# Query and key products of the first two batches straight from the loaded float32 data, for eight of sixteen heads

## The chip, the cores and the metric
The kernel runs on one core of a Trainium2 chip. Its time is device microseconds of one execution. The kernel before was timed three times; in addition, one execution was recorded by the hardware profiler, and all rows shown here come from that one.

## The reference
x is 8 batches of 128 tokens by 128 features, float32; ctx_1024 has the same shape. The computation is one decoder layer with layer norm behind each of its three parts:

```python
x = _layernorm(x + attn(x, w_q, w_k, w_v, w_o))             # 16 heads of 64, causal softmax(q k' / 8) v
x = _layernorm(x + xattn(x, ctx, mask, Wq..bo))             # 16 heads of 8, masked
x = _layernorm(x + ffn(x, router_w, w_gate, w_up, w_down))  # 8 experts, top 2, silu(gate) * up
```

The change touches only the first lines of the self-attention: `q = einsum(x, w_q)`, `k = einsum(x, w_k)`, `v = einsum(x, w_v)`, with weights of 1024 columns each (16 heads of 64), and the scale 1/8 of the scores, which the kernel multiplies into the query weights.

## The kernel before
All five engines run straight lists of instructions, written out by hand; semaphores tie them together, and there is no planner. TensorE works through its list in order, so what stands in front of an instruction delays it.

**Split products.** A product of x with the projection weights is made of three products in a rounded format. A float32 array a is held as a_hi, a rounded to the format float32r, and a_lo = a - a_hi. `split_product` (line 1441) adds hi*hi, lo*hi and hi*lo in one bank of PSUM. The three weight matrices are split in nine parts, `W_PARTS` (line 62): for each of the four column ranges of 256 (`W_COLS`) the query and then the key part, and last the value matrix as a whole. ScalarE makes the hi half with the scale in it (`round_w`, line 512, counted by `w_hi_done`), VectorE the lo half (`lower_w`, line 803, counted by `w_lo_done`), which reads the raw and the hi array in SBUF. GpSimd splits x pair by pair of batches (`split_x`, line 284).

**Loads.** SyncE issues xT of the first pair, one key part, three query parts, the value weights (line 254), the rest of xT (line 255), ctx and smaller ones; ScalarE issues the other weight parts (lines 508 to 510). Behind all lowerings (line 269) SyncE issues the gate and up weights, which overwrite the raw projection weights.

**The opening on TensorE** (from line 1609): ten float32 matmuls on a zeroed tile (`WARM`), then `first_qk(p)` for p = 0 to 7: q and k of two heads for the first pair of batches, each over 256 tokens, in one bank. `score_s(0, 0)`, the scores of eight heads of batch 0, stands behind `first_qk(5)`; it needs `first_qk(0)` to `(3)` copied out. Then follow `first_qk(6)`, `project_v(0, 0)`, `first_qk(7)`, `next_qk(0, 0)`, `project_v(0, 1)`, `next_qk(0, 2)`, `next_qk(0, 3)` and `score_s(0, 1)`. `next_qk(n, i)` is the same product for the next pair. Where a bank of PSUM is taken again, TensorE waits for its reader: `first_qk(7)` for `group_max("s", 0, 0)`, and `score_s(0, 1)` for `evac_v(0, 1)`.

**The copies out of PSUM.** ScalarE copies `first_qk` with even p (`evac_first_qk`, line 532), VectorE those with odd p (line 897). VectorE's list in this stage is: `lower_w(0)` to `(7)`, copies 1 and 3, `lower_w(8)`, two `group_max` (line 831, four masked reductions each), `evac_v(0, 0)`, copy 5, a reciprocal, copy 7, `evac_v(0, 1)`. ScalarE's is: `round_w(0)` to `(7)`, copies 0 and 2, `round_w(8)`, copy 4, a DMA issue, and the exponentials. GpSimd's is: `split_x(0)`, `split_x(1)`, `round_ctx(0)`, `split_x(2)`, `split_x(3)`, and then normalisations of the probabilities (line 311).

Of the kernel before, what the change touches and what calls it, by code (L numbers as in the profile page):

```python
# [38 lines left out]
def build_decoder(nc, x, xT, ctxT, mask, wqT, wkT, wvT, woT, cwqT, cwkT, cwvT, cwoT, cbq, cbk, cbv, cbo,  # L39
# [19 lines left out]


    W_COLS = (slice(0, 256), slice(256, 512), slice(512, 768), slice(768, 1024))
    W_PARTS = [(i, cols) for cols in W_COLS for i in (0, 1)] + [(2, slice(0, 1024))]
    NWP = len(W_PARTS)
    WARM = 10
    W_SCALE = (DQ ** -0.5, 1.0, 1.0)


# [6 lines left out]
    with ExitStack() as ctx:  # L74
# [3 lines left out]
        def sem(name):  # L78
            return ctx.enter_context(nc.semaphore(name))
# [130 lines left out]
        def hid_of(b):  # L210
            return max((j + 1 for j in range(NFILL) if FILL_BANK[j] is b), default=0)

        ld_xT, ld_xT_rest, ld_wv, ld_cwk, ld_cwq, ld_x, ld_ctx, ld_mask, ld_wo, ld_cw, ld_gu, ld_down = [
            sem(f"ld_{n}") for n in "xT xT_rest wv cwk cwq x ctx mask wo cw gu down".split()]
        stored, consts, pad_set, mask_set, w_hi_done, w_lo_done, gu_split, x_split, ctx_hi_done, ctx_lo_done, cwk_ready, cwq_ready, bias_step, bias_then_mean = [
            sem(n) for n in ("stored consts pad_set mask_set w_hi_done w_lo_done gu_split x_split ctx_hi_done ctx_lo_done cwk_ready cwq_ready "
                             "bias_step bias_then_mean").split()]
# [1 line left out]
            sem(n) for n in "qk_first qk_first_a qk_first_v kc_proj kc_evac kc_lower cv_proj cv_evac k_own_done cvp_done".split()]  # L219
        qk_proj, qk_evac = [[sem(f"{n}{i}") for i in range(4)] for n in ("qk_proj", "qk_evac")]  # L220
        v_proj, v_evac = [[sem(f"{n}{i}") for i in range(2)] for n in ("v_proj", "v_evac")]
        ld_wqk = [sem(f"ld_w{'qk'[i]}{k}") for k in range(len(W_COLS)) for i in (0, 1)]
        scored = {"s": [sem(f"scored_s{a}") for a in range(2)], "c": [sem(f"scored_c{j}") for j in range(NG)]}
        maxed, exped, turned, turned_evac = [{k: [sem(f"{n}_{k}{g}") for g in range(NG)] for k in "sc"}
                                             for n in ("maxed", "exped", "turned", "turned_evac")]
# [22 lines left out]
        @block.sync  # L248
        def _(sp):
            sp.dma_start(xT_all[:, 0:2 * S], xT[:, 0:2 * S]).then_inc(ld_xT, 16)  # L250
            sp.dma_start(w_raw[:, 1, W_COLS[0]], wkT[:, W_COLS[0]]).then_inc(ld_wqk[1], 16)
            for k in range(1, len(W_COLS)):
                sp.dma_start(w_raw[:, 0, W_COLS[k]], wqT[:, W_COLS[k]]).then_inc(ld_wqk[2 * k], 16)
            sp.dma_start(w_raw[:, 2, :], wvT).then_inc(ld_wv, 16)
            sp.dma_start(xT_all[:, 2 * S:B * S], xT[:, 2 * S:B * S]).then_inc(ld_xT_rest, 16)
            sp.dma_start(ctxT_all[:], ctxT).then_inc(ld_ctx, 16)
            sp.dma_start(cwqk_raw[:, 1], cwkT).then_inc(ld_cwk, 16)
            sp.dma_start(cwv_sb[:], cwvT).then_inc(ld_cw, 16)
            sp.dma_start(cwo_sb[:], cwoT).then_inc(ld_cw, 16)
            sp.dma_start(cb[:, 0], cbq).then_inc(ld_cw, 16)  # L260
            sp.dma_start(cb[:, 1], cbk).then_inc(ld_cw, 16)
            sp.dma_start(part[:], parts).then_inc(ld_cw, 16)
            sp.dma_start(cbrow[:, 0, :], cbv.rearrange("(a d) -> a d", a=1).broadcast_to([P, D])).then_inc(ld_cw, 16)
            sp.dma_start(cbrow[:, 1, :], cbo.rearrange("(a d) -> a d", a=1).broadcast_to([P, D])).then_inc(ld_cw, 16)
            sp.dma_start(router_sb[:], routerT).then_inc(ld_cw, 16)
            sp.dma_start(cwqk_raw[:, 0], cwqT).then_inc(ld_cwq, 16)
            sp.dma_start(wo_sb[:], woT).then_inc(ld_wo, 16)

            sp.wait_ge(w_lo_done, NWP)
            sp.dma_start(gu_raw[:, 0, :], gateT).then_inc(ld_gu, 16)  # L270
            sp.dma_start(gu_raw[:, 1, :], upT).then_inc(ld_gu, 16)
            sp.wait_ge(k_own_done, B)
            sp.dma_start(down_sb[:], down).then_inc(ld_down, 16)

            for c in range(NCH):
                for tb in range(TB):
                    b = c * TB + tb
                    sp.wait_ge(y_ready, b + 1)
                    sp.dma_start(out[b], y_out[:, tb, :]).then_inc(stored, 16)
            sp.wait_ge(stored, 16 * B)  # L280

        @block.gpsimd
        def _(pool):
            def split_x(k):
                toks = slice(2 * k * S, 2 * (k + 1) * S)
                pool.wait_ge(ld_xT if k == 0 else ld_xT_rest, 16)
                pool.tensor_copy(x_hi[:, toks], xT_all[:, toks]).then_inc(x_split, 1)
                pool.wait_ge(x_split, 2 * k + 1)
                pool.tensor_tensor(x_lo[:, toks], xT_all[:, toks], x_hi[:, toks].bitcast(F32), ALU.subtract).then_inc(x_split, 1)
# [217 lines left out]
        def _(act):  # L507
# [2 lines left out]
                act.dma_start(w_raw[:, 1, W_COLS[k]], wkT[:, W_COLS[k]]).then_inc(ld_wqk[2 * k + 1], 16)  # L510

            def round_w(part_of):
                i, cols = W_PARTS[part_of]
                act.wait_ge((*ld_wqk, ld_wv)[part_of], 16)
                act.activation(w_hi[:, i, cols], w_raw[:, i, cols], ACT.Copy, scale=W_SCALE[i]).then_inc(w_hi_done, 1)

            def exp(kind, g, n):
# [14 lines left out]
            def evac_first_qk(p, b):  # L532
                act.wait_ge(qk_first, p + 1)
                dst = qk_b[:, :, p % 4, :] if p >= 4 else qk_a[:, 0, :, p, :]
                act.copy(dst, b[:].rearrange("p (a c) -> p a c", a=2)).then_inc(qk_first_a, 1)

            def evac_qk(n, i, b):
                act.wait_ge(qk_proj[i], n + 1)
# [49 lines left out]
            def rank_exp():  # L588
                act.wait_ge(r_exp_in, 1)
                act.activation(r_a[:, 4:6].rearrange("p a b e -> p (a b e)"),  # L590
                               r_a[:, 0:2].rearrange("p a b e -> p (a b e)"), ACT.Exp).then_inc(r_exp, 1)

            round_w(0)
            round_w(1)
            round_w(2)
            round_w(3)
            round_w(4)
            round_w(5)
            round_w(6)
            round_w(7)  # L600
            evac_first_qk(0, Y1)
            evac_first_qk(2, T0)
            round_w(8)
            evac_first_qk(4, Y0)
            act.dma_start(mask_all, mask.rearrange("b q t -> q b t")).then_inc(ld_mask, 16)
            exp("s", 0, 0)
# [191 lines left out]
        def _(dve):  # L798
# [2 lines left out]
            dve.memset(cvp[:, :, :, DC:DC + 1], 1.0).then_inc(pad_set, 1)  # L801

            def lower_w(part_of):
                i, cols = W_PARTS[part_of]
                dve.wait_ge(w_hi_done, part_of + 1)
                dve.scalar_tensor_tensor(out=w_lo[:, i, cols], in0=w_raw[:, i, cols], scalar=W_SCALE[i],
                                         in1=w_hi[:, i, cols].bitcast(F32), op0=ALU.mult,
                                         op1=ALU.subtract).then_inc(w_lo_done, 1)
# [88 lines left out]
            def evac_first_qk(p, b):  # L897
                dve.wait_ge(qk_first, p + 1)
                dst = qk_b[:, :, p % 4, :] if p >= 4 else qk_a[:, 0, :, p, :]
                dve.tensor_copy(dst, b[:].rearrange("p (a c) -> p a c", a=2)).then_inc(qk_first_v, 1)  # L900

            def evac_qk(n, i, b):
                dve.wait_ge(qk_proj[i], n + 1)
# [139 lines left out]
            def rank_9():  # L1043
                step(tt(hot1, hot1, wide(z1), ALU.mult))
                step(tt(hot2, hot2, wide(z2), ALU.mult))
                tt(dense_w[:], hot1, hot2, ALU.add).then_inc(dense_ready, 1)

            lower_w(0)
            lower_w(1)
            lower_w(2)  # L1050
            lower_w(3)
            lower_w(4)
            lower_w(5)
            lower_w(6)
            lower_w(7)
            evac_first_qk(1, OS)
            evac_first_qk(3, T1)
            lower_w(8)
            dve.wait_ge(consts, 3)
            group_max("s", 0, 0, Y1)  # L1060
            group_max("s", 1, 0, T1)
            evac_v(0, 0, OS)
            evac_first_qk(5, X0)
            reciprocal_s(0, 0)
# [375 lines left out]
        def _(pe):  # L1440
# [11 lines left out]
                return last  # L1452

            def first_qk(p, b):
                if p == 0:

                    for a in range(2):
                        dst, cols = b[:, a * 2 * S:(a + 1) * 2 * S], slice(0, P)
                        pe.wait_ge(w_hi_done, a + 1)
                        pe.wait_ge(x_split, 1)  # L1460
                        pe.matmul(dst, w_hi[:, a, cols], x_hi[:, 0:2 * S], start=True, stop=False)
                        pe.wait_ge(x_split, 2)
                        pe.matmul(dst, w_hi[:, a, cols], x_lo[:, 0:2 * S], start=False, stop=False)
                        pe.wait_ge(w_lo_done, a + 1)
                        last = pe.matmul(dst, w_lo[:, a, cols], x_hi[:, 0:2 * S], start=False, stop=True)
                    last.then_inc(qk_first, 1)
                    return
                if p % 2 == 0:
                    pe.wait_ge(w_lo_done, p + 2)
                project_qk(0, p, b).then_inc(qk_first, 1)  # L1470

            def next_qk(n, i, b):
# [645 lines left out]
```

## Time and profile before

| | us |
|---|---|
| median of three runs | 233.56 (233.28 to 233.65) |
| the profiled execution: time / span | 233.06 / 231.0 |
| TensorE busy in the span | 225.9 (98%) |
| VectorE / ScalarE / GpSimd busy | 192.1 / 164.9 / 102.0 |

The span runs from the first to the last instruction of the program; the time of the same execution holds 2.06 us more around it. The profile's page says in how much of the span each engine was busy, and which line's work made up the chain that ended last. A float32 matmul stands in the trace as two records (the ten opening matmuls are 20 records), a float32r matmul as one. The granted share of TensorE's clock is 1.00 in every stretch of the run.

### The profile page before, as it was taken

What the parts mean: (1) busy time and instruction counts of PE and PEld (TensorE: products, weight loads), DVE (VectorE), ACT (ScalarE), POOL (GpSimd) and SP (SyncE); (2) the same over time, 40 slices, a digit from 0 to 9 for tenths busy, and PEclk for the clock granted to TensorE, in tenths of its full rate; (3) what the DMA queues carried; (4) which work ended last, traced back from release to release, by engine and by line L of the source; (5) the groups of instructions that cost most, each with busy time, mean ns of one, the idle gap of its engine ahead of it and who ended that gap; (6) DMA issues with size and microseconds to landing.
All of it is one profiled execution on the core that took longest, in us unless ns stands there. A gap on an engine that the chain in (4) does not pass through costs nothing.

```text
span 231.0 us, 6982 instructions
## 1 busy us (share of the span) xinstructions
PE 225.9 (98%) x2274; PEld 205.9 (89%) x2274; DVE 192.1 (83%) x954; ACT 164.9 (71%) x552; POOL 102.0 (44%) x162
## 2 busy tenths in 40 slices
PE   8999999999999999999999999999999999999992
PEld 8999888997978988978978988789999999999992
DVE  3897798997889889989899879989898565766984
ACT  3768988898999979999989999697476333333001
POOL 4387738796396568922978351231200000100112
PEclk9999999999999999999999999999999999999999
DMA  6998000000000000000002200000000000000000
GB/s 189 362 363 314 10 0 0 4 3 1 3 1 3 0 6 3 0 3 1 1 4 64 121 3 3 3 0 4 0 3 0 1 3 0 4 23 0 26 23 24
DMA packets 7011, 9.10 MB, mean 39 GB/s; under 512 B 1088, under 2 KB 5824, under 8 KB 6592
## 3 DMA queue, kind: packets, MB, share of 16 engines
q1 hardware_dynamic: 4320, 7.09, 8.7%
q10 hardware_dynamic: 2656, 1.57, 2.3%
q8 instruction: 18, 0.29, 0.5%
q14 instruction: 17, 0.14, 0.2%
HBM read 8.14 MB, written 0.52 MB: 37 GB/s over the span
## 4 chain that ended last, share of the span: by engine, by line
PE 96%; DVE 1%; issue 1%; POOL 1%; ACT 0%; POOLq 0%; ACTq 0%; DVEq 0%
PE bank L1545 13%; PE bank L1443 11%; PE bank L1445 10%; PE bank L1444 10%; PE bank L2043 9%; PE bank L1527 7%; PE bank L1554 7%; PE bank L1595 6%; PE bank L1563 4%; PE bank L1538 3%; PE bank L1611 2%; PE bank L1482 2%; PE bank L1483 2%; PE bank L1484 2%; PE bank L1570 2%; PE bank L2053 1%
## 5 line engine op out<-in xcount | busy, mean ns | idle before, releaser
L525 ACT ACTIVATE probs_s<-masked_s,nmax_s 128x128 f32<-128x128 f32 x128 | 49.8, 396 | 3.6 <-DVE nmax_s L839 2.1
L311 POOL TENSOR_TENSOR probs_s<-probs_s,rec_sum_s 128x512 f32<-128x512 f32 x32 | 33.1, 1040 | 35.0 <-DVE rec_sum_s L846 34.8
L586 ACT ACTIVATE silu<-bank 128x256 f32<-128x256 f32 x54 | 20.1, 384 | 30.3 <-PE bank L1445 28.4
L528 ACT ACTIVATE probs_c<-masked_c,nmax_c 128x128 f32<-128x128 f32 x128 | 40.3, 396 | 1.6 <-DVE nmax_c L839 1.4
L1443 PE MATMUL bank<-ctx_hi,gu_hi 128*128 128x256 f32 x128 | 38.7, 302 | 0.0
L1444 PE MATMUL bank<-ctx_lo,gu_hi 128*128 128x256 f32 x128 | 35.7, 279 | 0.0
L1445 PE MATMUL bank<-ctx_hi,gu_lo 128*128 128x256 f32 x128 | 35.7, 279 | 0.0
L839 DVE CUSTOM_DVE_ANT_0 masked_c<-bank,mask_add 128x128 f32<-128x128 f32 x128 | 29.0, 286 | 4.6 <-PE bank L1538 3.9
L839 DVE CUSTOM_DVE_ANT_0 masked_s<-bank,causal 128x128 f32<-128x128 f32 x128 | 29.2, 285 | 1.2 <-PE bank L1527 1.0
L503 POOL TENSOR_TENSOR mv<-mv,minus_half 128x1 f32<-128x1 f32 x7 | 3.8, 556 | 55.2 <-DVE mv L1388 55.2
L1443 PEld LDWEIGHTS bank<-ctx_hi,gu_hi 128*128 128x128 f32 x128 | 24.3, 190 | 0.7 <-DVE qk_a L969 0.3
L525 ACT ACTIVATION_READ_ACCUMULATOR probs_s<-masked_s,nmax_s 128x1 f32 x128 | 24.8, 193 | 0.0
L1444 PEld LDWEIGHTS bank<-ctx_lo,gu_hi 128*128 128x128 f32 x128 | 24.1, 188 | 0.0
L1445 PEld LDWEIGHTS bank<-ctx_hi,gu_lo 128*128 128x128 f32 x128 | 24.0, 188 | 0.0
L567 ACT COPY xT_all<-bank 128x512 f32<-128x512 f32 x32 | 17.8, 580 | 2.6 <-PE bank L1545 1.5
L1545 PE MATMUL bank<-ident,probs_c 128*128 128x128 f32 x128 | 18.8, 275 | 0.0
L1545 PE MATMUL bank<-ident,probs_s 128*128 128x128 f32 x128 | 18.7, 276 | 0.0
L1443 PE MATMUL bank<-x_hi,w_hi 128*128 128x256 f32 x62 | 18.2, 293 | 0.0
L969 DVE TENSOR_TENSOR qk_a<-silu,bank 128x256 f32<-128x256 f32 x32 | 12.7, 419 | 6.5 <-ACT silu L586 6.2
L1554 PE MATMUL bank<-probsT_s,v_sb 128*64 128x128 f32 x256 | 17.5, 279 | 0.0
L1445 PE MATMUL bank<-x_hi,w_lo 128*128 128x256 f32 x62 | 17.3, 279 | 0.0
L1444 PE MATMUL bank<-x_lo,w_hi 128*128 128x256 f32 x62 | 17.3, 279 | 0.0
(180 smaller groups left out, 591.4 us busy)
## 6 DMA issues: line engine op xcount, KB each, us to landing
raw<-in_gateT SPq DMA_DIRECT2D x1, 1024.0 KB, 8.2
raw<-in_upT SPq DMA_DIRECT2D x1, 1024.0 KB, 12.1
down_sb<-in_down SPq DMA_DIRECT2D x1, 1024.0 KB, 5.2
raw<-in_wvT SPq DMA_DIRECT2D x1, 512.0 KB, 5.6
ctxT_all<-in_ctxT SPq DMA_DIRECT2D x1, 512.0 KB, 6.9
masked_c<-in_mask ACTq DMA_DIRECT2D x1, 512.0 KB, 11.9
wo_sb<-in_woT SPq DMA_DIRECT2D x1, 512.0 KB, 6.1
x_tok<-in_x ACTq DMA_DIRECT2D x1, 512.0 KB, 11.2
```

Source lines behind the costliest of these rows:

```text
L311: pool.tensor_tensor(probs_s[:, g % 2], probs_s[:, g % 2], spread(rec_sum_s[:, 4 * g:4 * g + 4], 2, S), ALU.mult).then_inc(normed[g], 1)
L525: last = act.activation(probs_s[:, g % 2, i, :], masked_s[:, g % 2, i, :], ACT.Exp, scale=-1.0, bias=nmax_s[:, h:h + 1], accum_out=rsum_s[ ...
L528: last = act.activation(probs_c[:, g % 2, i, :], masked_c[:, g % 2, i, :], ACT.Exp, scale=-1.0, bias=nmax_c[:, h:h + 1])
L567: act.copy(dst[:, g % 2].rearrange("p h t -> p (h t)"), b[:]).then_inc(turned_evac[kind][g], 1)
L586: act.activation(silu[:, i % NS, :], g, ACT.Silu).then_inc(silued, 1)
L839: last = dve.tensor_tensor_reduce(out=masked[:, g % 2, i, :], in0=b[:, i * S:(i + 1) * S], in1=add, scale=-1.0, scalar=3e38, op0=ALU.add, ...
L1443: pe.matmul(dst, wh, xh, start=True, stop=False)
L1444: pe.matmul(dst, wh, xl, start=False, stop=False)
L1445: return pe.matmul(dst, wl, xh, start=False, stop=True)
L1545: last = pe.transpose(b[:, i * S:(i + 1) * S], (probs_s if kind == "s" else probs_c)[:, g % 2, i, :], ident[:])
L1554: last = pe.matmul(b[DQ * r:DQ * (r + 1), i * S:(i + 1) * S], v_sb[:, 8 * a + 2 * i + r, :], probsT_s[:, r, i, :], start=True, stop=True)
L2043: last = pe.matmul(down_bank(ce)[:, tb * P:(tb + 1) * P], hid[c % 2][:, e * FB + fb, tb * P:(tb + 1) * P], down_sb[:, e * FB + fb, :], sta ...
```

## The change
`first_qk(0)` to `(3)`, the query and key products of eight heads, become two float32 matmuls each on `w_raw` and `xT_all`, without splits; the scale goes into the copy of the query half, so each of these copies becomes two instructions of 256 columns. The parts are split in another order: column ranges 2 and 3 first, then 0 and 1, then the value matrix in two halves (ten parts). The opening matmuls go from ten to seven. The next pair's x gets a load of its own, in front of the value weights. The copies move in the lists of ScalarE and VectorE, and the second half of the value matrix is lowered behind two `group_max`.

```diff
-    W_PARTS = [(i, cols) for cols in W_COLS for i in (0, 1)] + [(2, slice(0, 1024))]
+    W_PARTS = [(i, k) for k in (2, 3, 0, 1) for i in (0, 1)] + [(2, 0), (2, 1)]
+    NDIRECT = 4
+    def w_cols(i, k):
+        return W_COLS[k] if i < 2 else slice(512 * k, 512 * (k + 1))
-    WARM = 10
+    WARM = 7
...
# SyncE
+            sp.dma_start(xT_all[:, 2 * S:4 * S], xT[:, 2 * S:4 * S]).then_inc(ld_xT_next, 16)
             sp.dma_start(w_raw[:, 2, :], wvT).then_inc(ld_wv, 16)
-            sp.dma_start(xT_all[:, 2 * S:B * S], xT[:, 2 * S:B * S]).then_inc(ld_xT_rest, 16)
+            sp.dma_start(xT_all[:, 4 * S:B * S], xT[:, 4 * S:B * S]).then_inc(ld_xT_rest, 16)
...
             sp.wait_ge(w_lo_done, NWP)
+            sp.wait_ge(qk_first, NDIRECT)
             sp.dma_start(gu_raw[:, 0, :], gateT).then_inc(ld_gu, 16)
# GpSimd, split_x
-                pool.wait_ge(ld_xT if k == 0 else ld_xT_rest, 16)
+                pool.wait_ge((ld_xT, ld_xT_next, ld_xT_rest, ld_xT_rest)[k], 16)
# ScalarE, round_w and evac_first_qk
+                act.wait_ge(ld_wqk[2 * k + i] if i < 2 else ld_wv, 32 if i < 2 and k >= 2 else 16)
...
+                if p < NDIRECT:
+                    act.activation(dst[:, 0], b[:, 0:2 * S], ACT.Copy, scale=W_SCALE[0])
+                    act.copy(dst[:, 1], b[:, 2 * S:4 * S]).then_inc(qk_first_a, 1)
# ScalarE's list
+            evac_first_qk(0, Y1)
             round_w(0)
...
             round_w(3)
+            evac_first_qk(2, T0)
             round_w(4)
...
             round_w(7)
-            evac_first_qk(0, Y1)
-            evac_first_qk(2, T0)
             round_w(8)
+            round_w(9)
             evac_first_qk(4, Y0)
# VectorE, evac_first_qk
+                if p < NDIRECT:
+                    dve.tensor_scalar(dst[:, 0], b[:, 0:2 * S], W_SCALE[0], None, ALU.mult)
+                    dve.tensor_copy(dst[:, 1], b[:, 2 * S:4 * S]).then_inc(qk_first_v, 1)
# VectorE's list
+            evac_first_qk(1, OS)
             lower_w(0)
...
             lower_w(3)
-            lower_w(4)
...
-            lower_w(7)
-            evac_first_qk(1, OS)
             evac_first_qk(3, T1)
-            lower_w(8)
+            for part_of in range(4, NWP - 1):
+                lower_w(part_of)
             dve.wait_ge(consts, 3)
             group_max("s", 0, 0, Y1)
             group_max("s", 1, 0, T1)
+            lower_w(NWP - 1)
             evac_v(0, 0, OS)
# TensorE, first_qk
+                if p < NDIRECT:
+                    if p == 0:
+                        pe.wait_ge(ld_xT, 16)
+                    for i in range(2):
+                        if p % 2 == 0:
+                            pe.wait_ge(ld_wqk[p + i], 16)
+                        last = pe.matmul(b[:, i * 2 * S:(i + 1) * 2 * S], w_raw[:, i, p * P:(p + 1) * P], xT_all[:, 0:2 * S],
+                                         start=True, stop=True)
                     last.then_inc(qk_first, 1)
                     return
+                if p == NDIRECT:
+                    pe.wait_ge(x_split, 2)
                 if p % 2 == 0:
-                    pe.wait_ge(w_lo_done, p + 2)
+                    pe.wait_ge(w_lo_done, p - NDIRECT + 2)
# TensorE, project_v
-                    pe.wait_ge(w_lo_done, NWP)
+                    pe.wait_ge(w_lo_done, NWP - 1 + c)
```

## Rows read from the trace of the kernel before

**Rows 1.** The page: busy engines; shares of the chain that ended last.

```profile
PE 225.9 (98%) x2274; PEld 205.9 (89%) x2274; DVE 192.1 (83%) x954; ACT 164.9 (71%) x552; POOL 102.0 (44%) x162
PE 96%; DVE 1%; issue 1%; POOL 1%; ACT 0%; POOLq 0%; ACTq 0%; DVEq 0%
```

**Rows 2.** Timeline of TensorE, 0 to 20 us: start, us, engine, line, operation, tiles.

```profile
0.98 4.64 PE L1611 MATMUL bank<-x 128*128 128x128 f32 x20 [0.98 <-POOL x L381]
...
5.62 0.31 PE L1463 MATMUL bank<-x_lo,w_hi 128*128 128x256 f32 x1
...
8.51 0.28 PE L1443 MATMUL bank<-x_hi,w_hi 128*128 128x256 f32 x1
...
9.21 0.28 PE L1443 MATMUL bank<-x_hi,w_hi 128*128 128x256 f32 x1
...
10.00 1.16 PE L1527 MATMUL bank<-qk_a 64*128 64x128 f32 x16
...
16.20 1.16 PE L1527 MATMUL bank<-qk_b 64*128 64x128 f32 x16
...
17.79 1.95 PE L1497 MATMUL bank<-cwv_sb,ctxT_all 128*128 128x128 f32 x16
```

**Rows 3.** Timeline of ScalarE, 0 to 12 us.

```profile
3.92 0.42 ACT L515 ACTIVATE w_hi<-raw 128x256 fp32r<-128x256 f32 x1
...
5.74 2.06 ACT L515 ACTIVATE w_hi<-raw 128x256 fp32r<-128x256 f32 x6 [0.70 <-DMA raw<-in_wqT]
7.70 1.05 ACT L535 COPY qk_a<-bank 128x512 f32<-128x512 f32 x2
8.64 1.07 ACT L515 ACTIVATE w_hi<-raw 128x1024 fp32r<-128x1024 f32 x1
```

**Rows 4.** Timeline of VectorE, 0 to 16 us.

```profile
4.37 1.23 DVE L806 SCALAR_TENSOR_TENSOR w_lo<-raw,w_hi 128x256 fp32r<-128x256 f32 x2 [2.27 <-ACT w_hi L515]
6.19 2.15 DVE L806 SCALAR_TENSOR_TENSOR w_lo<-raw,w_hi 128x256 fp32r<-128x256 f32 x6 [0.58 <-ACT w_hi L515]
8.25 1.28 DVE L900 COPY qk_a<-bank 128x512 f32<-128x512 f32 x2
9.74 1.36 DVE L806 SCALAR_TENSOR_TENSOR w_lo<-raw,w_hi 128x1024 fp32r<-128x1024 f32 x1 [0.21 <-ACT w_hi L515]
11.33 0.29 DVE L839 CUSTOM_DVE_ANT_0 masked_s<-bank,causal 128x128 f32<-128x128 f32 x1 [0.23 <-PE bank L1527]
...
13.03 0.69 DVE L915 COPY v_sb<-bank 128x512 f32<-128x512 f32 x1
...
14.90 0.69 DVE L915 COPY v_sb<-bank 128x512 f32<-128x512 f32 x1
```

**Rows 5.** Timeline of GpSimd, 3 to 15 us.

```profile
4.26 0.73 POOL L289 TENSOR_TENSOR x_lo<-xT_all,x_hi 128x256 fp32r<-128x256 f32 x1
...
10.10 1.59 POOL L289 TENSOR_TENSOR x_lo<-xT_all,x_hi 128x256 fp32r<-128x256 f32 x1
...
13.83 0.74 POOL L289 TENSOR_TENSOR x_lo<-xT_all,x_hi 128x256 fp32r<-128x256 f32 x1
```

**Rows 6.** DMA issues by line: queue, count, KB, us from issue to landing.

```profile
raw<-in_wqT SPq DMA_DIRECT2D x3, 128.0 KB, 4.3
...
xT_all<-in_xT SPq DMA_DIRECT2D x1, 128.0 KB, 3.0
raw<-in_wkT SPq DMA_DIRECT2D x1, 128.0 KB, 3.4
```

**Rows 7.** Timeline of all engines: DMA issues of SyncE.

```profile
1.16 0.43 SPq L251 DMA_DIRECT2D raw<-in_wkT  x1
...
1.63 1.37 SPq L253 DMA_DIRECT2D raw<-in_wqT  x3
```

**Rows 8.** Timeline of all engines, 22 to 24 us: the last normalisation of batch 0 and its reader.

```profile
22.21 1.04 POOL L311 TENSOR_TENSOR probs_s<-probs_s,rec_sum_s 128x512 f32<-128x512 f32 x1 [0.76 <-DVE rec_sum_s L846]
...
23.11 0.86 PEld L1545 LDWEIGHTS bank<-ident,probs_s 128*128 128x128 f32 x8 [0.17 <-issue]
```

More of the change, by code:

```diff
@@ L211, in hid_of @@
             return max((j + 1 for j in range(NFILL) if FILL_BANK[j] is b), default=0)
-        ld_xT, ld_xT_rest, ld_wv, ld_cwk, ld_cwq, ld_x, ld_ctx, ld_mask, ld_wo, ld_cw, ld_gu, ld_down = [
-            sem(f"ld_{n}") for n in "xT xT_rest wv cwk cwq x ctx mask wo cw gu down".split()]
+        ld_xT, ld_xT_next, ld_xT_rest, ld_wv, ld_cwk, ld_cwq, ld_x, ld_ctx, ld_mask, ld_wo, ld_cw, ld_gu, ld_down = [
+            sem(f"ld_{n}") for n in "xT xT_next xT_rest wv cwk cwq x ctx mask wo cw gu down".split()]
         stored, consts, pad_set, mask_set, w_hi_done, w_lo_done, gu_split, x_split, ctx_hi_done, ctx_lo_done, cwk_ready, cwq_ready, bias_step, bias_then_mean = [
@@ L221, in build_decoder @@
         v_proj, v_evac = [[sem(f"{n}{i}") for i in range(2)] for n in ("v_proj", "v_evac")]
-        ld_wqk = [sem(f"ld_w{'qk'[i]}{k}") for k in range(len(W_COLS)) for i in (0, 1)]
+        ld_wqk = [sem(f"ld_w{'qk'[i]}{k}") for k in range(2) for i in (0, 1)]
+        for k in (2, 3):
+            ld_wqk += 2 * [sem(f"ld_wqk{k}")]
         scored = {"s": [sem(f"scored_s{a}") for a in range(2)], "c": [sem(f"scored_c{j}") for j in range(NG)]}
@@ L512, in round_w @@
             def round_w(part_of):
-                i, cols = W_PARTS[part_of]
-                act.wait_ge((*ld_wqk, ld_wv)[part_of], 16)
+                i, k = W_PARTS[part_of]
+                cols = w_cols(i, k)
+                act.wait_ge(ld_wqk[2 * k + i] if i < 2 else ld_wv, 32 if i < 2 and k >= 2 else 16)
                 act.activation(w_hi[:, i, cols], w_raw[:, i, cols], ACT.Copy, scale=W_SCALE[i]).then_inc(w_hi_done, 1)
@@ L534, in evac_first_qk @@
                 dst = qk_b[:, :, p % 4, :] if p >= 4 else qk_a[:, 0, :, p, :]
-                act.copy(dst, b[:].rearrange("p (a c) -> p a c", a=2)).then_inc(qk_first_a, 1)
+                if p < NDIRECT:
+                    act.activation(dst[:, 0], b[:, 0:2 * S], ACT.Copy, scale=W_SCALE[0])
+                    act.copy(dst[:, 1], b[:, 2 * S:4 * S]).then_inc(qk_first_a, 1)
+                else:
+                    act.copy(dst, b[:].rearrange("p (a c) -> p a c", a=2)).then_inc(qk_first_a, 1)
             def evac_qk(n, i, b):
@@ L803, in lower_w @@
             def lower_w(part_of):
-                i, cols = W_PARTS[part_of]
+                i, cols = W_PARTS[part_of][0], w_cols(*W_PARTS[part_of])
                 dve.wait_ge(w_hi_done, part_of + 1)
@@ L899, in evac_first_qk @@
                 dst = qk_b[:, :, p % 4, :] if p >= 4 else qk_a[:, 0, :, p, :]
-                dve.tensor_copy(dst, b[:].rearrange("p (a c) -> p a c", a=2)).then_inc(qk_first_v, 1)
+                if p < NDIRECT:
+                    dve.tensor_scalar(dst[:, 0], b[:, 0:2 * S], W_SCALE[0], None, ALU.mult)
+                    dve.tensor_copy(dst[:, 1], b[:, 2 * S:4 * S]).then_inc(qk_first_v, 1)
+                else:
+                    dve.tensor_copy(dst, b[:].rearrange("p (a c) -> p a c", a=2)).then_inc(qk_first_v, 1)
             def evac_qk(n, i, b):
@@ L1051, in _ @@
             lower_w(3)
-            lower_w(4)
-            lower_w(5)
-            lower_w(6)
-            lower_w(7)
-            evac_first_qk(1, OS)
             evac_first_qk(3, T1)
-            lower_w(8)
+            for part_of in range(4, NWP - 1):
+                lower_w(part_of)
             dve.wait_ge(consts, 3)
@@ L1454, in first_qk @@
             def first_qk(p, b):
[L1455 to L1465, printed above, removed]
+                if p < NDIRECT:
[6 more added lines that the diff above has]
+                                         start=True, stop=True)
                     last.then_inc(qk_first, 1)
                     return
+                if p == NDIRECT:
+                    pe.wait_ge(x_split, 2)
                 if p % 2 == 0:
-                    pe.wait_ge(w_lo_done, p + 2)
+                    pe.wait_ge(w_lo_done, p - NDIRECT + 2)
                 project_qk(0, p, b).then_inc(qk_first, 1)
```

## The prediction
> **What bounds the kernel now.** I read the page first: TensorE is busy in 98% of the span and carries 96% of the chain that ended last [rows 1]. So what counts is TensorE's list: what is added to it, what is taken out, and where it comes to a wait. Everything the change touches lies in the first 17 us, so next I read the timelines of the four engines there. TensorE opens with 20 records of float32 matmuls on zeros, from 0.98 to 5.62, and at 5.62 the first real products are under way [rows 2]. From then on it has no long pause: `score_s(0, 0)` starts at 10.00 and `score_s(0, 1)` at 16.20 [rows 2]. I take 16.20 as the gauge: the wait that ended last there tells the cost, because behind it TensorE's list is unchanged and nearly full. VectorE is the other one to watch. From 11.33 to its copy of the second half of v at 14.90 it runs without a pause [rows 4], and `score_s(0, 1)` needs that copy (done at 14.90 + 0.69 = 15.59). It has 0.6 us to spare.
>
> **The pace of each kind of work.**
> - From 0.98 to the record at 5.62 lie 20 opening records and one real product: 4.64 / 21 = 0.221 each. A record of 128 float32 columns takes that at the low level of the clock (1.2 GHz). From 5.62 on the steps are about half as long, the high level (2.4 GHz).
> - Float32 at the high level: a record is shown 0.16 longer than its step (0.28 against 0.12 at 8.51), so 16 records of 128 columns in 1.95 are (1.95 - 0.16) / 16 = 0.112 each [rows 2].
> - No row shows a float32 matmul of 256 columns. From above: two records with twice the columns, so four times 0.112 = 0.448. From below: float32r passes of 256 columns, of which six take 9.21 - 8.51 = 0.70, 0.117 each [rows 2]; two of them would be 0.23. A matmul of two cheaper records would save TensorE 1 us here, and the wait named below would hide that. I take 0.448, because the float32 rows bear on it and the step grows with the columns.
> - A direct `first_qk` is then 2 x 0.448 = 0.90 against 0.70 for the split one. Four of them add 0.8 us to TensorE (between -0.95 and +0.8).
> - VectorE: six lowerings of 256 columns from 6.19 to 8.25, 0.343 each; a copy of 512 columns 1.28 - 0.69 = 0.59, say 0.60; a `group_max` half of 13.03 - 11.33, 0.85; v, copy 5, reciprocal and copy 7 together 14.90 - 13.03 = 1.87 [rows 4]. A copy in two halves: between 0.60 (no fixed part) and 0.86 (each as long as a whole lowering's record, 0.43); I take 0.68, two lowering steps. A lowering of 512 columns: between 0.61 and 0.69, half of 1.36 or two of 0.343 less a fixed part; I take 0.64.
> - ScalarE: roundings of 256 columns (7.70 - 5.74) / 6 = 0.33; copies of 512 (8.64 - 7.70) / 2 = 0.47 [rows 3]. Halved copies: 0.47 to 0.66; I take 0.54.
>
> **TensorE alone.** Three opening matmuls fewer are 6 records less: the opening ends at 0.98 + 14 x 0.221 = 4.08. The first q weights have landed by 3.92, where ScalarE rounds them [rows 3]. x is issued by SyncE some 0.43 in front of the first k weights (at 1.16) and lands 3.0 later, at about 3.7; those land at 1.16 + 3.4 = 4.56 [rows 6, 7]. So nothing holds the start. `first_qk(0)` runs at the low clock: q to 4.96, k to 5.75 (its last record is partly behind 5.6). Then 0.90 each: 6.64, 7.54, 8.43. The second column range has landed by then (three loads issued from 1.63 on, median 4.3 to landing) [rows 6, 7]. Two split ones end at 9.83, and `score_s(0, 0)` can start at 9.91 against 10.00. So on TensorE alone the 1.3 us of earlier start pay for the dearer products and for the low clock, and hardly a tenth is left. The result is set by who hands over late.
>
> **VectorE's list, which I expect to be late.** `evac_first_qk(1)` now stands first. Product 1 ends at 6.64, its result comes 0.16 later (record 0.28 less step 0.12), and with 0.05 for the handover the copy starts at 6.86. The rest follows without a pause: copy 1 to 7.54; four lowerings to 8.91; copy 3 (product 3 has been out since 8.6) to 9.59; four lowerings to 10.96; the first half of v's weights to 11.60; `group_max` to 12.45 and 13.30; the second half of v's weights to 13.94; v, copy 5, reciprocal, copy 7 to 15.81; the second v copy done at 15.81 + 0.69 = 16.50. `score_s(0, 1)` starts at 16.54: **+0.34**. On the way TensorE has small waits that this one swallows: `score_s(0, 0)` at 9.91 meets copy 3 (done 9.67); `project_v(0, 0)` waits for 11.67, `first_qk(7)` for 12.5, `project_v(0, 1)` for 14.0.
>
> ScalarE is not the late one: copy 0 from 5.97 to 6.5, four roundings to 7.8, copy 2 to 8.4, four roundings to 9.7, two halves of v to about 10.8 [paces of rows 3]; each rounding is out 0.5 us or more before VectorE takes it up. The v weights, which had landed by 8.64 [rows 3], come about 0.35 later for the 128 KB put in front of them: still ahead of 9.7. Copy 4 moves from 9.6 to 11, and the exponentials don't start before 12.5, so it is hidden. The gate and up loads go out at 14.0 instead of 11.1, behind the tenth lowering; the wait for four products passes long before. GpSimd splits them only behind the normalisations of batches 0 and 1: no cost. The further SyncE issue (0.43) delays small loads by as much, also unused before 17 us. I put all these at nothing.
>
> **The meetings with GpSimd.** The trace shows VectorE's lowerings and GpSimd's subtractions stopping each other. Two lowerings at 4.37 take 1.23 where two steps make 0.76: 0.47 too much, while `x_lo` runs from 4.26 to 4.99 [rows 4, 5]. At 10.10 `x_lo` takes 1.59 instead of 0.73, until a lowering from 9.74 to 11.10 has let go. Who starts second waits. In the kernel before only the first meeting costs VectorE anything, and at a time when it is ahead. In the new one x of the next pair lands behind the weight parts, not behind v: by estimate at 7.3 (the third load of L253 at 2.6 + 4.3 = 6.9, and a quarter of the 1.7 to 8.64 that 512 KB of v took at most). So its subtraction falls at about 7.9 to 8.6, into the first four lowerings. The last pair's was at 13.83 [rows 5]; with `split_x(1)` out of its way it comes some 0.6 earlier, 13.2 to 13.9, on the tenth lowering. And all of this now stands in the row of work without a pause. Price of a meeting: nothing where VectorE is first, 0.47 where GpSimd is. Three may happen (the third is the ninth lowering with `round_ctx(0)`); I take one at full price.
>
> The Trainium skill says in "SBUF — State Buffer", section "SBUF: two separate sides", that VectorE and GpSimd share a pair of ports as an exclusive lock, also against VectorE operations with two SBUF inputs, and that the one who comes second is blocked entirely. The two rows above agree with it. By this rule alone, each lowering behind which GpSimd waits could lose a whole subtraction (0.73), and the sum would be +1.1 in place of +0.8.
>
> **Sum.** +0.34 + 0.47 = +0.8 us. The profiled execution took 233.06, so it would take 233.9; the median of the runs is 0.5 above the profiled one, so I give 233.56 + 0.8 = 234.4.
>
> **The rivals.**
> 1. *No meeting costs VectorE anything* (it streams its lowerings and GpSimd stays the second): +0.34, 233.9. For it: at 10.10 it went that way. Against: at 4.37 it did not.
> 2. *The clock rises earlier, as the real products start* (the side of not slower). Then product 0 takes 0.90 and ends at 4.99, product 1 at 5.88, and VectorE starts at 6.10. The rounding it needs is tied to the load of the third column range, the second of the three loads at L253: about 2.1 + 4.3 = 6.4, plus 0.42, so the first lowering starts at 6.82 instead of 7.54. VectorE's whole row comes 0.72 earlier: +0.34 - 0.72 = -0.38, 233.2. It decides from the point where the rise comes 0.5 us before 5.6. For it: a float32 matmul of 256 columns cheaper than 0.448 works in the same direction. Against: both levels are seen only behind 20 records on zeros, and TensorE's work is as gapless now as before.
> 3. *Several meetings and a late follow-up.* VectorE is 0.9 late at 15.8 while TensorE is 0.3 late. With three meetings at 0.47 it comes to +1.75. On top, the last normalisation of batch 0 ends at 22.21 + 1.04 = 23.25 and its reader is in the pair of transposes that starts at 23.11, about 0.5 into it [rows 8]: 0.35 to spare, which a late VectorE eats. +1.9, 235.5.
> 4. *The clock stays at the low level through all direct products*: product 3 ends at 4.08 + 4 x 1.77 = 11.2 (0.90 x 0.221 / 0.112 = 1.77) in place of 8.43: +2.6 or so, 236. Against: in the trace it rises at 5.6 behind the same kind of matmul.
>
> **How the numbers follow.** Main case (one meeting, or as much in small parts) 0.42, rival 1 0.25, rival 2 0.17, rival 3 0.13, rival 4 0.03. 0.2% of 233.56 is 0.47 us, about what this measurement can tell from no change. The main case and rivals 3 and 4 lie above +0.47 save a tail of the first; rival 1 mostly within; rival 2 astride the lower bound. Faster 0.15, same 0.33, slower 0.52. Range 233.2 to 235.3: it takes in rivals 1 and 2 at their price and the main case with its bounds, and leaves out rival 4 and the upper part of 3. The main case's own range is 234.0 to 234.9.
>
> **What would show it.** Opening records 14, ending near 4.3; 16 records of 256 float32 columns for the direct products, about 0.22 apart once the clock is up; product 4 near 8.4; VectorE without a pause from about 6.9 to 16.5, with one lowering visibly longer than 0.43; `score_s(0, 1)` at 16.5 to 17.0, and its wait ended by VectorE. I am wrong if `score_s(0, 1)` starts before 16.2, if TensorE waits there for ScalarE or a load, or if the difference at 16.2 is not the difference at the end.

## The result: slower by 0.7%

| | before | after |
|---|---|---|
| median of 8 runs each, us | 233.53 (233.08 to 233.99) | 235.13 (234.44 to 235.95) |
| ratio | | 1.0069, 95% interval 1.0054 to 1.0085 |
| profiled execution: time / span | 233.06 / 231.0 | 235.18 / 233.3 |

Every ratio here leaves out the few executions in a slower state (one each of e3_both and e4_warm10, at most two of the kernel before).

The forecast was 234.4, with a range of 233.2 to 235.3. The measured 235.13 lies in that range, but above the main case's own range of 234.0 to 234.9. The sign was as forecast, and so were the place (the start of `score_s(0, 1)`, the gauge of the prediction) and the engine that TensorE waits for there (VectorE). The size was twice the forecast: 1.60 us where the sum gave 0.8.

The page of the changed kernel, to be read beside [rows 1]:

```profile
span 233.3 us, 6962 instructions
## 1 busy us (share of the span) xinstructions
PE 226.8 (97%) x2260; PEld 205.0 (88%) x2260; DVE 192.5 (82%) x957; ACT 164.8 (71%) x555; POOL 101.8 (44%) x162
```

TensorE is busy 0.9 us more, the span is 2.3 us longer: most of the loss is waiting. (These two executions lie 2.12 us apart in time, the medians 1.60.) Where, the timeline of TensorE says (start, duration, engine, line, idle before and what ended it), the counterpart of [rows 2]:

```profile
4.12 1.06 PE L1480 MATMUL bank<-xT_all,raw 128*128 128x256 f32 x2
5.38 3.68 PE L1480 MATMUL bank<-xT_all,raw 128*128 128x256 f32 x14 [0.20 <-DMA raw<-in_wkT]
9.64 0.36 PE L1461 MATMUL bank<-x_hi,w_hi 128*128 128x256 f32 x1 [0.58 <-DVE w_lo L822]
...
11.21 1.16 PE L1545 MATMUL bank<-qk_a 64*128 64x128 f32 x16
...
13.45 0.50 PE L1500 MATMUL bank<-w_hi,x_hi 128*128 128x512 f32 x1 [0.17 <-DVE w_lo L822]
...
18.20 1.16 PE L1545 MATMUL bank<-qk_b 64*128 64x128 f32 x16
```

The products start at 4.12 (forecast 4.08). Then TensorE waits for the first key weights, and later for VectorE's lowerings: product 4, forecast near 8.4, starts at 9.64. `score_s(0, 1)` starts at 18.20, 2.0 after [rows 2] and later than the 16.5 to 17.0 that the prediction named; the scores of batch 2 start at 34.17 where before they did at 32.17. The difference at the gauge stays. VectorE in the same stretch (counterpart of [rows 4]; L917, L918 are the copy in halves, L822 the lowerings, that is the making of the lo halves, L935 the v copies):

```profile
7.38 0.42 DVE L917 TENSOR_SCALAR qk_a<-bank 128x256 f32<-128x256 f32 x1 [5.28 <-PE bank L1480]
7.72 0.41 DVE L918 COPY qk_a<-bank 128x256 f32<-128x256 f32 x1
8.05 2.12 DVE L822 SCALAR_TENSOR_TENSOR w_lo<-raw,w_hi 128x256 fp32r<-128x256 f32 x4
10.09 0.41 DVE L917 TENSOR_SCALAR qk_a<-bank 128x256 f32<-128x256 f32 x1
...
10.76 2.63 DVE L822 SCALAR_TENSOR_TENSOR w_lo<-raw,w_hi 128x256 fp32r<-128x256 f32 x5
15.00 0.69 DVE L822 SCALAR_TENSOR_TENSOR w_lo<-raw,w_hi 128x512 fp32r<-128x512 f32 x1
...
17.48 0.67 DVE L935 COPY v_sb<-bank 128x512 f32<-128x512 f32 x1
```

VectorE has no idle time from 7.38 to the end of this v copy at 17.48 + 0.67 = 18.15, and TensorE goes on at 18.20. GpSimd beside it (counterpart of [rows 5]):

```profile
7.95 0.40 POOL L297 CAST x_hi<-xT_all 128x256 fp32r<-128x256 f32 x1 [3.26 <-DMA xT_all<-in_xT]
8.43 0.78 POOL L299 TENSOR_TENSOR x_lo<-xT_all,x_hi 128x256 fp32r<-128x256 f32 x1
11.48 0.83 POOL L304 CAST ctx_hi<-ctxT_all 128x512 fp32r<-128x512 f32 x1 [2.27 <-DMA ctxT_all<-in_ctxT]
12.26 0.59 POOL L297 CAST x_hi<-xT_all 128x256 fp32r<-128x256 f32 x1
12.93 1.06 POOL L299 TENSOR_TENSOR x_lo<-xT_all,x_hi 128x256 fp32r<-128x256 f32 x1
```

Each instruction of GpSimd between 7.95 and 12.9 overlaps a lowering. The first four lowerings take 2.12 instead of 1.42, the next five 2.63 instead of 2.02 (the undisturbed figures are those of e1_quiet below, where one lowering takes 0.42, and 0.68 with 512 columns). These four are the long ones, the first, second, eighth and ninth:

```profile
8.05 0.58 DVE L822 SCALAR_TENSOR_TENSOR w_lo<-raw,w_hi 128x256 fp32r<-128x256 f32 x1
8.55 0.95 DVE L822 SCALAR_TENSOR_TENSOR w_lo<-raw,w_hi 128x256 fp32r<-128x256 f32 x1
11.76 0.82 DVE L822 SCALAR_TENSOR_TENSOR w_lo<-raw,w_hi 128x256 fp32r<-128x256 f32 x1
12.51 0.88 DVE L822 SCALAR_TENSOR_TENSOR w_lo<-raw,w_hi 128x512 fp32r<-128x512 f32 x1
```

The second meets a subtraction (`x_lo`), the other three meet casts (`x_hi`, `ctx_hi`, `x_hi`). The subtraction at 12.93 waits itself, 1.06 instead of 0.74, and costs VectorE nothing.

### The profile page after: what moved, and what is told of

It reads as the page before. It is cut to its first block, busy times and chain, and to the rows that moved or that the text cites. A ratio compares the mean times of both kernels' runs of the same rounds, so it can differ in the third digit from the quotient of the medians.

```text
span 233.3 us, 6962 instructions
## 1 busy us (share of the span) xinstructions
PE 226.8 (97%) x2260; PEld 205.0 (88%) x2260; DVE 192.5 (82%) x957; ACT 164.8 (71%) x555; POOL 101.8 (44%) x162
## 4 chain that ended last, share of the span: by engine, by line
PE 90%; DVE 5%; DMA 2%; issue 1%; POOL 0%; ACT 0%; POOLq 0%; SPq 0%; ACTq 0%
PE bank L1563 13%; PE bank L1461 9%; PE bank L2061 9%; PE bank L1462 9%; PE bank L1463 9%; PE bank L1572 7%; PE bank L1545 7%; PE bank L1613 6%; PE bank L1581 4%; PE bank L1556 3%; PE bank L2071 2%; DVE w_lo L822 2%; DMA raw<-in_wkT 2%; PE bank L1500 2%; PE bank L1588 2%; PE bank L1501 1%
## 5 line engine op out<-in xcount | busy, mean ns | idle before, releaser
L1461 PE MATMUL bank<-x_hi,w_hi 128*128 128x256 f32 x56 | 16.6, 296 | 0.6 <-DVE w_lo L822 0.6
L330 POOL TENSOR_TENSOR k_own<-down_sb,own 128x512 fp32r<-128x512 f32 x16 | 16.3, 1039 | 0.0
L1572 PEld LDWEIGHTS bank<-probsT_s,v_sb 128*64 128x64 f32 x256 | 13.6, 136 | 2.7 <-issue 1.5
```

Source lines behind the costliest of these rows:

```text
L1461: pe.matmul(dst, wh, xh, start=True, stop=False)
L1572: last = pe.matmul(b[DQ * r:DQ * (r + 1), i * S:(i + 1) * S], v_sb[:, 8 * a + 2 * i + r, :], probsT_s[:, r, i, :], start=True, stop=True)
```

## Experiments

Each ratio is against runs of the kernel before on the same chip; the gauge of a run is the start of `score_s(0, 1)` in its one trace. Theory A: VectorE's row sets `score_s(0, 1)`, and the meetings with GpSimd lengthened it. Theory B: TensorE's dearer list is the loss, wherever the waits are.

**e1_quiet.** GpSimd is kept off the lowerings.

```diff
             split_x(0)
+            pool.wait_ge(w_lo_done, NWP - 1)
             split_x(1)
+            pool.wait_ge(w_lo_done, NWP)
             round_ctx(0)
-            split_x(2)
-            split_x(3)
             normalise(0, 0)
             normalise(1, 0)
+            split_x(2)
+            split_x(3)
```

> GpSimd stays off VectorE's lowerings: the second split of x waits for nine lowerings, the ctx rounding for ten, and the last two splits of x stand behind two normalisations. Nothing on TensorE, ScalarE or VectorE changes. Theory A (VectorE's row without a pause sets score_s(0, 1), and meetings with GpSimd lengthened it by 1.2 us: 0.67 in the first four lowerings, 0.38 in the next four, 0.17 in the ninth): every 256-column lowering takes 0.41 to 0.43, score_s(0, 1) starts at 16.9 to 17.1 instead of 18.20, time 1.0 to 1.3 us less, about 234.0. Theory B (the four float32 products cost TensorE 0.7 us, and the rest is lost later): no change, 235.1.

Measured: 234.95 us, ratio 1.0071 (1.0057 to 1.0086). By the time alone, theory B would have won. VectorE's timeline:

```profile
6.95 0.42 DVE L919 TENSOR_SCALAR qk_a<-bank 128x256 f32<-128x256 f32 x1 [4.86 <-PE bank L1482]
...
7.63 1.42 DVE L824 SCALAR_TENSOR_TENSOR w_lo<-raw,w_hi 128x256 fp32r<-128x256 f32 x4
...
9.63 2.02 DVE L824 SCALAR_TENSOR_TENSOR w_lo<-raw,w_hi 128x256 fp32r<-128x256 f32 x5
```

The two groups are 0.70 and 0.61 shorter, together 1.31, and the row starts 0.43 earlier, since here the key weights held nothing up. TensorE's timeline in the same run:

```profile
16.46 1.16 PE L1547 MATMUL bank<-qk_b 64*128 64x128 f32 x16
...
24.08 0.63 PE L1565 MATMUL bank<-ident,probs_s 128*128 128x128 f32 x4 [0.64 <-POOL probs_s L321]
25.08 0.63 PE L1565 MATMUL bank<-ident,probs_s 128*128 128x128 f32 x4 [0.37 <-POOL probs_s L321]
```

`score_s(0, 1)` starts at 16.46, which is 1.74 earlier than 18.20: 1.31 + 0.43. So A holds at the gauge. Then 1.2 us are given back: the moved splits stand in front of the normalisations of heads 8 to 15, and the transposes wait for those.

**e2_copy5.** VectorE's row is made shorter in another way.

```diff
# ScalarE's list
             evac_first_qk(4, Y0)
+            evac_first_qk(5, X0)
# VectorE's list
             evac_v(0, 0, OS)
-            evac_first_qk(5, X0)
...
# TensorE, score_s
-                    pe.wait_ge(qk_first_a, 2 * a + 2)
-                    pe.wait_ge(qk_first_v, 2 * a + 2)
+                    pe.wait_ge(qk_first_a, (2, 5)[a])
+                    pe.wait_ge(qk_first_v, (2, 3)[a])
...
```

> The copy of product 5 moves from VectorE (0.58 us in its row) to ScalarE, which idles 2.5 us before its first exponential. GpSimd as in the changed kernel. Theory A: VectorE's row is 0.6 us shorter behind evac_v(0, 0), score_s(0, 1) starts at about 17.6, time 0.5 to 0.6 us less, about 234.5. Theory B: no change, 235.1.

Measured: 234.50, ratio 1.0053 (1.0037 to 1.0069), 0.4 us under the changed kernel's ratio, and `score_s(0, 1)` at 17.79. Nothing that TensorE executes was changed. The direction is A's; the intervals of the two ratios overlap. GpSimd is as in the changed kernel, and in this trace it lengthened the lowerings as much: the first four take 2.16, the next five 2.63.

**e3_both.** The edits of e1_quiet and e2_copy5 together.

> Both edits of the two runs before together. Theory A: the gains add up until TensorE's own list is the bound: score_s(0, 1) at 16.3 to 16.6, time 233.4 to 233.9, within 0.2% of the kernel before. Theory B: no change, 235.1.

Measured: 234.22, ratio 1.0038 (1.0025 to 1.0052); `score_s(0, 1)` at 16.48, batch 2 at 33.24. The gauge is as A says, the time is not (233.4 to 233.9 was expected): 0.8 us are given back at the same place as in e1_quiet.

**e4_warm10.** The changed kernel with ten opening matmuls.

```diff
-    WARM = 7
+    WARM = 10
```

> The changed kernel with ten opening matmuls instead of seven: the products start 1.3 us later, at about 5.4. Theory A with the profiled landing of the first key weights at 5.3: product 0 runs at the high clock throughout and ends at 6.3 as before, so that the earlier start bought nothing: score_s(0, 1) at 18.2, 235.1 to 235.3. If the key weights as a rule land at 4.6, as in the trace of the kernel before, product 0 ends 0.5 later than with seven, and the time is 235.6. Theory B expects up to 1.3 us more, 236.4.

Measured: 235.65, ratio 1.0095 (1.0074 to 1.0117): 0.6 us dearer than with seven, though the intervals of the two ratios overlap. Its trace is of a quick execution (234.91) and has the gauge at 17.75, so it does not show the 0.6; the lowerings are lengthened there too (the first four take 1.96, the next five 2.63). That the key weights as a rule are not as late as in the profiled execution of the changed kernel is better seen in the traces: of the ten with seven opening matmuls, only that one has TensorE waiting for them. So the 0.43 us that they cost there are probably no part of the 1.60 between the medians.

**e5_quiet2.** As e1_quiet, but `split_x(2)` and `split_x(3)` stand behind `key_bias()`.

> As e1_quiet, but the last two splits of x stand behind the key bias, where GpSimd idles 3.6 us, and no longer in front of the normalisations of heads 8 to 15 of batch 0, for which TensorE waited in e1_quiet (1.22 us between 22.3 and 25.5). Theory A (the gain of 1.7 us at score_s(0, 1) was given back there): score_s(0, 1) at 16.5 to 16.9 and the score of batch 2 also within 0.1 of +0.3 to +0.6 against the kernel before; time 233.8 to 234.1. Theory B (TensorE's dearer products, wherever the waits are): 234.9 to 235.1 again.

Measured: 234.55, ratio 1.0060 (1.0042 to 1.0079), not the 233.8 to 234.1 that A gave. I had misplaced GpSimd's idle time by one normalisation. GpSimd and TensorE in this run:

```profile
28.57 2.04 POOL L321 TENSOR_TENSOR probs_s<-probs_s,rec_sum_s 128x512 f32<-128x512 f32 x2
32.53 1.04 POOL L321 TENSOR_TENSOR probs_s<-probs_s,rec_sum_s 128x512 f32<-128x512 f32 x1 [1.92 <-DVE rec_sum_s L864]
```

```profile
16.02 1.16 PE L1547 MATMUL bank<-qk_b 64*128 64x128 f32 x16
...
29.76 0.63 PE L1565 MATMUL bank<-ident,probs_s 128*128 128x128 f32 x4 [0.51 <-POOL probs_s L321]
30.76 0.63 PE L1565 MATMUL bank<-ident,probs_s 128*128 128x128 f32 x4 [0.37 <-POOL probs_s L321]
```

At the gauge this kernel is 0.18 ahead of the kernel before, and it stays so until 28.15 (28.33 in the kernel before). Behind the two late normalisations of batch 1 it is 0.93 behind (scores of batch 2 at 33.10).

**e6_quiet2_copy5.** e5_quiet2 with copy 5 on ScalarE.

> e5_quiet2 with the copy of product 5 on ScalarE. Theory A: VectorE's row is no longer the bound at score_s(0, 1), TensorE's own list is: 16.3 to 16.5, and nothing lost later: 233.6 to 233.8, no difference from the kernel before that can be told. Theory B: 234.5 or more.

Measured: 234.38, ratio 1.0043 (1.0027 to 1.0059), with the same waits for GpSimd (233.6 to 233.8 was expected). In its trace TensorE's steps halve only at 7.1, and the gauge is at 16.88.

**e7_direct_only.** The kernel before with the four direct products and their split copies, and nothing else of the change.

> The kernel before with one part of the change alone: products 0 to 3 directly in float32, with their copies in halves; ten opening matmuls, order of the splits, lists and loads as before. It prices TensorE's part by itself: 16 records of 0.216 us against 24 of 0.117, +0.7 us, at score_s(0, 1) (16.9) and at the end: 234.1 to 234.3. Both theories expect that; a rival (the cheaper waits hide it, since the float32 products wait for no split) expects 233.5.

Measured: 233.78, ratio 1.0025 (1.0012 to 1.0039), +0.6 us. The part of the change that costs TensorE work costs 0.6 by itself, by the times. Its one trace does not show it: it is of a quick execution (233.30) in which the clock rose early, at 4.8, and the gauge is at 16.27 where 16.9 was expected. In the full change the three opening matmuls less pay for the 0.6, as e4_warm10 indicates from the other side with the same 0.6.

**e9_quiet3_copy5.** As e6_quiet2_copy5, with the two splits behind `normalise(0, 1)`.

> As e6_quiet2_copy5, with the last two splits of x one place further, behind the second normalisation of batch 1, where the trace of e5_quiet2 has GpSimd's idle time (1.92 us left of 3.3). In e5_quiet2 the gain at score_s(0, 1) held until 28.1 and was given back (1.1 us) to the two normalisations that stood behind the moved splits. Theory A: the difference to the kernel before at score_s(0, 1), between -0.2 and +0.7 with the moment at which the clock rises (4.8 to 7.1 us in the traces so far), is the difference at the end: 233.6 to 233.9. Theory B (TensorE's dearer products plus something later): 234.4 again.

Measured: 233.75, ratio 1.0011 (0.9997 to 1.0025). TensorE's timeline, and its waits over the whole run (the only one is that for the first constant):

```profile
16.05 1.16 PE L1547 MATMUL bank<-qk_b 64*128 64x128 f32 x16
...
29.20 1.09 PE L1565 MATMUL bank<-ident,probs_s 128*128 128x128 f32 x8
...
32.01 1.16 PE L1547 MATMUL bank<-qk_a 64*128 64x128 f32 x16
```

```profile
PE bank L1631 <- POOL x L391: 1.0, 1, 1.0
```

This kernel has the change's loads, opening, direct products, halved copies and order of the splits, and TensorE works through the same list. Only GpSimd's order, its two waits and the engine of one copy differ. 1.3 us of the 1.6 are gone. That settles it against B. It does not settle how the 1.3 divide: e2_copy5 puts 0.4 on the copy, which would leave some 0.9 for GpSimd if the two add up (an estimate), and GpSimd's new order without the moved copy was not run.

**e8_two_direct.** A cheaper use of the idea: only products 0 and 2 direct, seven opening matmuls, splits and loads as in the kernel before.

> A version that may beat both: the kernel before with products 0 and 2 alone direct, and seven opening matmuls; all splits, lists and loads as before. Product 0 runs at the low clock from 4.1 to 5.8, product 1 split to 6.5, product 2 direct without its wait for a split to 7.35, product 3 to 8.05, product 4 at 8.05 where it was 8.40. score_s(0, 1) at 15.9 instead of 16.20: 233.2. If the key weights land at 5.3, half of that is lost. A rival (the early float32 product at the low clock gains nothing) expects 233.5 or more.

Measured: 233.23, ratio 1.0000 (0.9987 to 1.0012). Product 4 starts at 8.10 (8.05 expected), but `score_s(0, 0)` waits for VectorE's copy 3 (9.93), and the ninth lowering meets `x_lo` and takes 1.71 us. The gauge is at 16.49, where 15.9 was expected: no gain is left there.

**e10_two_direct_quiet.** e8_two_direct, with GpSimd out of the way.

```diff
             split_x(0)
+            pool.wait_ge(w_lo_done, NWP)
             split_x(1)
             round_ctx(0)
             split_x(2)
-            split_x(3)
             normalise(0, 0)
...
             normalise(0, 1)
+            split_x(3)
# VectorE's list
             lower_w(3)
+            evac_first_qk(1, OS)
...
             lower_w(7)
-            evac_first_qk(1, OS)
```

> e8_two_direct with GpSimd kept off the lowerings (in e8 its subtraction made the ninth lowering 1.71 us long instead of 1.36, and score_s(0, 0) waited for VectorE's copy 3), and copy 1 in VectorE's gap behind four lowerings. Theory A: score_s(0, 0) at 9.6, VectorE's row then from 11.3 as in the kernel before, second v copy done at 15.55, score_s(0, 1) at 15.7 to 15.9 instead of 16.20: 233.0, 0.3 to 0.5 under the kernel before. Theory B: no difference from e8_two_direct.

Measured: 233.09, ratio 0.9979 (0.9970 to 0.9988). It is faster than both kernels, by 0.5 us against the one before. Its trace shows the undisturbed lowering, but an execution in which the clock rose late:

```profile
4.12 1.91 PE L1470 MATMUL bank<-xT_all,raw 128*128 128x256 f32 x4
5.47 0.78 PE L1453 MATMUL bank<-x_hi,w_hi 128*128 128x256 f32 x1
6.05 0.41 PE L1454 MATMUL bank<-x_lo,w_hi 128*128 128x256 f32 x1
6.26 0.41 PE L1455 MATMUL bank<-x_hi,w_lo 128*128 128x256 f32 x1
```

```profile
10.12 1.23 DVE L812 SCALAR_TENSOR_TENSOR w_lo<-raw,w_hi 128x1024 fp32r<-128x1024 f32 x1 [0.29 <-ACT w_hi L517]
```

Steps of 0.21 for 256 float32r columns at 6.05 are the low level; in the first trace of the kernel before, the step at that point was 0.12. So `score_s(0, 1)` at 16.50 in this trace (15.7 to 15.9 expected) shows no gain; the time of eleven runs does.

**e11_two_direct_best.** e10_two_direct_quiet with copy 5 on ScalarE.

> e10_two_direct_quiet with the copy of product 5 on ScalarE: VectorE's row 0.6 shorter, TensorE's own list the bound. score_s(0, 1) at 15.6 to 15.7: 232.9, 0.5 under the kernel before. If e10 is already bound by TensorE there, no difference from it.

Measured: 233.43, ratio 0.9998 (0.9986 to 1.0009). A miss: it is 0.2% slower than e10_two_direct_quiet. VectorE's row has gaps now, so it was no longer the bound. Why the shorter row costs something I did not find out. In the two traces 0.37 us of the difference lie behind TensorE's last product (the span ends 4.54 after it, against 4.17); whether that is the cause, one trace of each can't tell.

**b0_before.** The kernel before, traced once more.

> The kernel before once more, for a second trace of it: whether the clock's rise (5.7 us) and the landing of the first key weights (4.6) move from execution to execution as they do in the changed kernels (4.8 to 7.1; 4.6 to 5.4), and whether score_s(0, 1) moves with them. If the kernel before is as sensitive, score_s(0, 1) lies off 16.20 by half the shift of the rise; time 233.5.

Measured: ratio 0.9990 (0.9972 to 1.0008); the profiled execution took 233.73. Its timelines of TensorE, ScalarE, VectorE and GpSimd:

```profile
7.74 0.38 PE L1443 MATMUL bank<-x_hi,w_hi 128*128 128x256 f32 x1 [0.77 <-DVE w_lo L806]
...
16.95 1.16 PE L1527 MATMUL bank<-qk_b 64*128 64x128 f32 x16
```

```profile
6.47 2.04 ACT L515 ACTIVATE w_hi<-raw 128x256 fp32r<-128x256 f32 x6 [1.80 <-DMA raw<-in_wqT]
```

```profile
10.46 1.75 DVE L806 SCALAR_TENSOR_TENSOR w_lo<-raw,w_hi 128x1024 fp32r<-128x1024 f32 x1 [0.21 <-ACT w_hi L515]
```

```profile
10.39 0.74 POOL L289 TENSOR_TENSOR x_lo<-xT_all,x_hi 128x256 fp32r<-128x256 f32 x1
```

The second column range landed at 6.47 instead of 5.74 [rows 3], and the gauge moved by 0.75. With the load late, the ninth lowering met GpSimd's subtraction as the second and took 1.75 instead of the undisturbed 1.23. The kernel before is as open to a late load as the changed one, and has meetings of its own. A gauge from a single trace is good to some 0.75 us here.

## Why the prediction was right, and where it was half the size

- **TensorE alone breaks even: right, as far as the times tell.** The direct records follow at 0.216 each (forecast 0.224), product 4 could have started at 8.9. e7_direct_only and e4_warm10 price the two halves at 0.6 each, forecast 0.7 to 0.8 against 1.3 less the low clock.
- **VectorE's row is what ends last: right.** Its end at 18.15 releases `score_s(0, 1)` at 18.20, its pieces are as forecast (a halved copy 0.67, half a v part 0.61), and the edits that shorten it bring the gauge forward. The base of +0.34 came out as +0.26 in e1_quiet's trace (16.46 against 16.20), where no lowering is lengthened and no load late; in e5_quiet2's, where the clock rose early, at about 5.0, as -0.18.
- **The meetings: the term that was mis-sized.** I took one at 0.47. The changed kernel's trace had four instructions of GpSimd on the lowerings, and against e1_quiet they cost 1.31; the traces of e2_copy5 and e4_warm10, with GpSimd's list unchanged, give 1.35 and 1.15. The 1.31 and the base of 0.34 make 1.65, and 1.60 was measured. That they agree so closely is partly luck: the gauge of that trace is off by 2.0, with the late key weights in it, and a single gauge is good to 0.75. Two points were wrong. I had three possible meetings and put one in the sum, and of the casts I counted only that of ctx; but casts lengthened three lowerings (by 0.16, 0.40 and 0.20), the subtraction one (by 0.53). And I priced a meeting at nothing where VectorE comes first, and expected that for most of them. A row of short instructions has an end every 0.34 us, and GpSimd got in at one of them each time. The meeting forecast on the tenth lowering cost nothing (0.69 against 0.68).
- **What the rows of before had to say on it.** I wrote that only the first meeting costs VectorE anything in the kernel before. The lowering at 9.74 [rows 4] takes 1.36, and 1.23 undisturbed (e10_two_direct_quiet), because a cast was ahead of it:

```profile
9.62 0.40 POOL L287 CAST x_hi<-xT_all 128x256 fp32r<-128x256 f32 x1 [4.63 <-DMA xT_all<-in_xT]
```

- **The page's rule** gave +1.1 as I worked it, with one whole subtraction (0.73) lost; the one subtraction that met a lowering cost 0.53, and the casts brought the rest. The Trainium skill, page "SBUF — State Buffer", section "SBUF: two separate sides", has a VectorE operation with two SBUF inputs exclude a GpSimd operation that reads SBUF, and makes no exception for a cast. The trace agrees: the casts held lowerings up as the subtraction did, with the 0.58, 0.82 and 0.88 above.
- **Nothing absorbs it later: right** to 0.1 us at batch 2. The span ended 0.3 more behind than that: it ends 4.52 after TensorE's last product, against 4.16 and 4.17 in the two traces of the kernel before. No run has an edit there, yet this tail is 4.17 in e8_two_direct and e10_two_direct_quiet and 4.35 to 4.54 in the traces of all other variants. So up to 0.4 of the difference may arise at the end of the kernel, and why stays open.
- **Rival 2** (an earlier rise of the clock) did not come about in the changed kernel's trace, where TensorE's steps halve between 6.0 and 6.3. But the moment moves: it lay at 4.8 to 7.1 us in the fourteen traces, at 4.8 to 5.7 in the four with ten opening matmuls and at 5.0 to 7.1 in the ten with seven. Whether the shorter opening makes the rise later as a rule, these few traces can't tell; the sum left that out. e9_quiet3_copy5 has the shorter opening too and is 0.3 us behind the kernel before in all, 0.6 at the upper end of its interval, so there it can hardly cost more. Rival 3's three meetings at 0.47 (1.41) are nearest to what happened, without its late follow-up.

## What to carry to other kernels

When an edit moves work out of one engine's way, look at what now stands in a row without a pause on another engine, and which third engine's instructions hold that one up. Price such meetings per instruction of the third engine, casts included, and not per likely collision. If a wait is removed and the time does not move, follow the gain along the trace to where it is given back: e1_quiet and e5_quiet2 were 1.7 and 2.2 us ahead of the changed kernel at the gauge and lost 1.2 and 1.1 of them again at two later points, and only the third place for the moved work lost nothing.

## What the runs showed of the hardware

- A float32 matmul stands in the trace as two records. At the high level of the clock they are 0.216 us apart with 256 columns (changed kernel) and 0.112 with 128 (kernel before), at the low level 0.427 and 0.213. A float32r matmul is one record, of 0.117 with 256 columns at the high level and 0.21 at the low one (e10_two_direct_quiet).
- A GpSimd cast, which has one SBUF input, lengthens a VectorE operation with two SBUF inputs as a subtraction does. A 128x256 lowering of 0.42 us took 0.58 and 0.82 beside casts and 0.95 beside a subtraction, a 128x512 one of 0.68 took 0.88 beside a cast (changed kernel), and a 128x1024 one of 1.23 (e10_two_direct_quiet) took 1.36 beside a cast (kernel before) and 1.71 and 1.75 beside a subtraction (e8_two_direct, b0_before).
- A row of VectorE's instructions without a pause did not keep GpSimd out: in the changed kernel four of its instructions got in ahead of a lowering, for 1.31 us in nine lowerings.
- TensorE started its matmuls at 0.97 to 0.98 in every one of the fourteen traces, and its steps halved, from the low level of the clock to the high one, at a point between 4.8 and 7.1.
- The same load of the same kernel released ScalarE at 5.74 in one execution and at 6.47 in another (kernel before and b0_before), and in the second the gauge was 0.75 us later.
